# The low halves of attention's probabilities, taken for two quarters of a head in one operation

## The chip, the cores and the metric

The kernel runs on one core of one Trainium2 chip. The metric is the device time of one execution in microseconds (us), as the median of three runs.

## The reference, cut to what matters

A two-layer network of four sequences of 512 rows with 512 features each. Of its stages the change touches one, the cross attention of the second layer (16 heads of 32 features, 1024 keys, 4 sequences):

```
scores = einsum('bhsd,bhtd->bhst', Q, K) * scale
attn   = softmax(scores, axis=-1)
ctx    = einsum('bhst,bhtd->bhsd', attn, V)
```

All is float32 in the reference. Before this stage come the keys and values of the context, a first attention, a mixture of ternary experts and the queries; behind it come the output projection and a second mixture of experts.

## The kernel before, in words

The stages follow one another, each in a block of its own; a stage begins when every engine has left the one before. The change is in `attention_phase` (L1436 to L1800). It works through 4 sequences x 16 heads = 64 heads, each in 4 quarters, 256 steps in all. A head has 512 queries and 1024 keys.

**Two views of the scores.** For the maxima TensorE computes the scores with the queries on the partitions (`max_scores`, L1706, two matmuls of 512 columns for one quarter of the queries, into one of two places of `t_psM`), and VectorE takes their maximum (`maximum`, L1670, 128x1024). For the softmax it computes them again with the keys on the partitions (`scores`, L1725, one matmul for each of the quarter's two blocks of 128 keys, into two places of `t_psE`), now with the maxima as three more rows of the contraction. ScalarE takes the exponential of each block (L1632) into `t_e`, float32, a ring of 8 quarters.

**High and low halves.** `mix` (L1736) multiplies the probabilities with the values in bfloat16. The high half of a float32 number is read in place (`upper`, every second 16-bit word of `t_e`). The low half, the number less its high half, is computed by the function `halves` into `t_low`, with a subtraction of 128x1024 for one quarter. Quarters u = 0 and 2 are taken by GpSimd (L1591), u = 1 and 3 by VectorE (L1678). `mix` of a quarter has four matmuls: for each block one on the high and one on the low half.

**Order.** It is written by hand. In the step (h, u) TensorE issues `max_scores` for the quarter 28 steps on (EARLY), then for each of two blocks `scores` of the quarter 4 steps on (AHEAD) and `mix` of (h, u): 8 matmuls a step. VectorE issues in the step first `halves` of the quarter 3 steps on, if that is one of its own, and then the maximum of the quarter 28 steps on. GpSimd issues `halves` of the quarter 4 steps on, if that is one of its own. In the last 28 steps (7 heads) there are no more maxima to compute. `wait_free` (L1530) makes TensorE's `max_scores` wait until the maximum of the quarter that held its place of `t_psM` has been taken, which is the one two steps back.

**Groups.** Every 16 steps (4 heads) GpSimd splits the maxima of a group in three bfloat16 parts (`max_parts`, L1601, L1603, L1605, L1607, in the step h = 1, u = 1 of each four heads, behind that step's `halves`), and TensorE turns them (`max_transpose`, L1714, in the step h = 2, u = 1 of each four heads, ahead of that step's `max_scores`). The turned block takes a place of `t_psM` for itself, so that the `max_scores` behind it waits for the maximum of the step just before.

**Waits of `halves`.** GpSimd waits until VectorE has written its half that comes before in the order of quarters (`lo_dve`), and for the exponentials (`expd`). VectorE waits for the exponentials alone. `mix` of a quarter waits for its low half (`wait_lo`, L1482).

Of the kernel before, what the change touches and what calls it, by code (L numbers as in the profile page):

```python
# [6 lines left out]
BF16 = mybir.dt.bfloat16  # L7
ACT = mybir.ActivationFunctionType
ALU = mybir.AluOpType
# [1426 lines left out]
def attention_phase(nc, queries_dram, keys_dram, values_dram, mixed_dram, ident, qst, loaded, kst, vst, kv_loaded, ones_set):  # L1436
# [8 lines left out]
    TC = T // P  # L1445
    AHEAD, MAXAHEAD = 4, 7
    RING = 8
    LO_ON_POOL = (0, 2)
    NLD = 3
    mixed_v = mixed_dram.rearrange("b r (h d) s -> b h r d s", h=NH)  # L1450

    with ExitStack() as c:
        sb = lambda name, shape, dt: c.enter_context(nc.sbuf_tensor(name, shape, dt))
        sem = lambda name: c.enter_context(nc.semaphore(name))
        e32 = sb("t_e32", [P, RING, 2, S], F32)
        low = sb("t_low", [P, RING, 2, S], BF16)
# [13 lines left out]
        scored, expd = sem("t_scored"), sem("t_expd")  # L1470
        lo_dve, lo_pool = sem("t_lo_dve"), sem("t_lo_pool")
# [1 line left out]
        copied_out = sem("t_copied_out")  # L1473
        stored = [sem(f"t_stored{i}") for i in range(2)]

        def upto(quarters, head, u):

            return head * len(quarters) + sum(q <= u for q in quarters)

        LO_ON_DVE = tuple(u for u in range(4) if u not in LO_ON_POOL)  # L1480

        def wait_lo(eng, head, u):  # L1482
            pool = u in LO_ON_POOL
            eng.wait_ge(lo_pool if pool else lo_dve, upto(LO_ON_POOL if pool else LO_ON_DVE, head, u))

        def slot(h, u):

            return (h * 4 + u) % RING

        def upper(h, u):  # L1490

            return e32[:, slot(h, u), :, :].rearrange("p i s -> p (i s)").bitcast(BF16).rearrange(
                "p (i s w) -> p i s w", i=2, w=2)[:, :, :, 1]

        def ahead(b, h, u, n):

            h, u = h + (u + n) // 4, (u + n) % 4
            return b + h // NH, h % NH, u

        def steps(b):  # L1500
            return [(b, h, u) for h in range(NH) for u in range(4)]
# [7 lines left out]
        def within(b, h):  # L1509

            return not (isinstance(b, int) and b > LAST)

        def place_of_max(b, m):

            after = (m - LATE) // GROUP
            return m + (max(0, after) if isinstance(b, int) and b == 0 else after)
# [5 lines left out]
        def banks_of(place):  # L1522

            return psM[:, place % 2, :, :]
# [17 lines left out]
        def group_at(b, h, u, step):  # L1542

            if (4 * h + u) % GROUP == step:
                b2, h2, _ = ahead(b, h // G * G, 0, GROUP)
                if within(b2, h2):
                    return b2, h2 // G
            return None

        with nc.Block() as block:  # L1550
            @block.sync
            def _(sp):
                def load(b, g):
                    load_queries(sp, b, g, queries_dram, qst, loaded)
                    load_keys_values(sp, b, g, keys_dram, values_dram, kst, vst, kv_loaded)

                def put_max(b, g):

                    sp.wait_ge(n_copied, b * G + g + 1)
                    sp.dma_start(qst[KR:AR, g, :, :].rearrange("r h (u s) -> r (h u) s", u=4),  # L1560
                                 nrows[:, :]).then_inc(max_loaded[g], 16)

                def batch(b):
                    for h in range(NH):
                        if h % G == 1 and (due := group_at(b, h - 1, 0, 0)):
                            put_max(*due)
                        sp.wait_ge(copied_out, b * NH + h + 3)
                        sp.dma_start(mixed_v[bass.ds(b, 1), h].rearrange("o r d s -> (o r) d s"),
                                     ost[:, h % 2, :]).then_inc(stored[h % 2], 16)
                        if h % G == G - 1 and not (isinstance(b, int) and b == LAST):  # L1570
                            sp.wait_ge(mixed, (b * NH + h) * 4 + 4 + RING)
                            load(b + 1, h // G)

                for i in range(2):
                    sp.sem_inc(stored[i], 16)
                put_max(0, 0)
                for b in range(B):
                    batch(b)
                for i in range(2):
                    sp.wait_ge(stored[i], 16 * (B * NH // 2 + 1))  # L1580

            @block.gpsimd
            def _(pool):
                def halves(b, h, u):
                    head = b * NH + h
                    if u in LO_ON_POOL:
                        before = upto(LO_ON_DVE, head, u)
                        if not (isinstance(before, int) and before == 0):
                            pool.wait_ge(lo_dve, before)
                        pool.wait_ge(expd, head * 8 + 2 * u + 2)  # L1590
                        nc.gpsimd.tensor_tensor(low[:, slot(h, u), :, :], e32[:, slot(h, u), :, :], upper(h, u),  # L1591
                                                ALU.subtract).then_inc(lo_pool, 1)

                def max_parts(b, g):

                    k = b * G + g
                    pool.wait_ge(maxed, k * GROUP + GROUP)
                    if not (isinstance(b, int) and b == 0 and g == 0):
                        pool.wait_ge(n_xposed, k)
                    m, zeros = nmax[:, g % 2, :, :], nparts[:, 3, :, :]  # L1600
                    nc.gpsimd.tensor_tensor(nparts[:, 0, :, :], m, zeros, ALU.subtract).then_inc(n1_done, 1)  # L1601
                    pool.wait_ge(n1_done, k + 1)
                    nc.gpsimd.tensor_tensor(nrest[:, :, :], m, nparts[:, 0, :, :], ALU.subtract).then_inc(nrest_done, 1)  # L1603
                    pool.wait_ge(nrest_done, k + 1)
                    nc.gpsimd.tensor_tensor(nparts[:, 1, :, :], nrest[:, :, :], zeros, ALU.subtract).then_inc(n2_done, 1)  # L1605
                    pool.wait_ge(n2_done, k + 1)
                    nc.gpsimd.tensor_tensor(nparts[:, 2, :, :], nrest[:, :, :], nparts[:, 1, :, :],  # L1607
                                            ALU.subtract).then_inc(n3_done, 1)

                nc.gpsimd.memset(nparts[:, :, :, :], 0.0).then_inc(zeros_set, 1)  # L1610
                pool.wait_ge(zeros_set, 1)
                max_parts(0, 0)
                for n in range(AHEAD):
                    halves(*ahead(0, 0, 0, n))
                def batch(b):
                    for _, h, u in steps(b):
                        b2, h2, u2 = ahead(b, h, u, AHEAD)
                        if within(b2, h2):
                            halves(b2, h2, u2)
                        if due := group_at(b, h, u, SPLIT_AT):  # L1620
                            max_parts(*due)
                for b in range(B):
                    batch(b)
# [41 lines left out]
            @block.vector  # L1665
            def _(dve):
                def maximum(b, h, u):
                    m = 4 * h + u
                    dve.wait_ge(max_scored, b * 4 * NH + m + 1)
                    nc.vector.tensor_reduce(nmax[:, h // G % 2, h % G, u:u + 1],  # L1670
                                            banks_of(place_of_max(b, m)).rearrange("p a t -> p (a t)"),
                                            AX_X, ALU.max, negate=True).then_inc(maxed, 1)

                def halves(b, h, u):
                    head = b * NH + h
                    if u in LO_ON_DVE:
                        dve.wait_ge(expd, head * 8 + 2 * u + 2)
                        nc.vector.tensor_tensor(low[:, slot(h, u), :, :], e32[:, slot(h, u), :, :], upper(h, u),  # L1678
                                                ALU.subtract).then_inc(lo_dve, 1)

                for m in range(EARLY):
                    maximum(*ahead(0, 0, 0, m))
                    if m >= EARLY - AHEAD + 1:
                        halves(*ahead(0, 0, 0, m - EARLY + AHEAD - 1))
                def batch(b):
                    for _, h, u in steps(b):
                        b2, h2, u2 = ahead(b, h, u, AHEAD - 1)
                        if within(b2, h2):
                            halves(b2, h2, u2)
                        b2, h2, u2 = ahead(b, h, u, EARLY)  # L1690
                        if within(b2, h2):
                            maximum(b2, h2, u2)
                for b in range(B):
                    batch(b)
# [666 lines left out]
```

## Time and profile before

| | |
|---|---|
| median of 3 runs | 1772.18 us (1770.33 to 1776.66) |
| the profiled execution | 1772.23 us, its span 1770.4 us |
| PE busy | 1454.6 us (82%), 8465 matmuls |
| DVE busy | 1258.1 us (71%) |
| ACT busy | 970.7 us (55%) |
| POOL busy | 438.6 us (25%) |
| the attention stage | 778.5 to 1277.4 us |
| of it, steps with maxima at full rate | 830 to 1237 us |
| steps without maxima | 1237 to 1277.4 us |

PE is TensorE, DVE VectorE, ACT ScalarE, POOL GpSimd, SP the queue that issues DMAs. A row of the timeline gives the start of an instruction, its duration, engine, line of the code, operation, and what it writes and reads; in square brackets stands how long the engine was idle before it and who released it. "x2" merges two in a row. Matmuls overlap: one of 512 columns is recorded with 0.38 us, while the next starts 0.22 us behind it. Two VectorE operations in a row overlap in the record by some 0.08 us: a pair of maxima is recorded with 2.34 us, one alone with 1.21.

### The profile page before, as it was taken

The numbers are of one execution on the slowest core, as the hardware profiler recorded it, in microseconds if no ns is written. First come the engines' busy times: TensorE is split into PE (matmuls) and PEld (weight loads), VectorE is DVE, ScalarE is ACT, GpSimd is POOL, SyncE is SP. The second block draws the span as 40 slices with busy tenths as digits, with TensorE's granted clock in tenths as the row PEclk, the third lists the DMA queues.
The fourth block names the chain that finished last, engine by engine and source line by source line (L and its number), as shares of the span: only waits on it lengthen the run. The fifth ranks groups of instructions, "written<-read, shape, count | busy, mean of one in ns | idle before, by whom it ended". The sixth has DMA issues, their size and how long they took to land. (4 is left out here: it accounts for less than half of the span.)

```text
span 1770.4 us, 24758 instructions
## 1 busy us (share of the span) xinstructions
PE 1454.6 (82%) x8465; PEld 839.6 (47%) x8536; DVE 1258.1 (71%) x1520; ACT 970.7 (55%) x1440; POOL 438.6 (25%) x343
## 2 busy tenths in 40 slices
PE   4999988999551774878999999999826599999996
PEld 3554534555240333323555555555403366666663
DVE  4888856655582676859999999999448686655551
ACT  5878723344171555414777777767612376665551
POOL 0122210000313004304555555555752000000000
PEclk9999998999755996878999999999958699999998
DMA  6788650000083226420423233331177396666640
GB/s 220 244 276 290 204 205 1 0 0 0 1 354 111 72 90 186 111 79 11 97 74 95 76 92 79 90 81 28 36 213 226 115 327 219 219 220 219 220 142 28
DMA packets 145938, 236.92 MB, mean 134 GB/s; under 512 B 11320, under 2 KB 61496, under 8 KB 144704
## 3 DMA queue, kind: packets, MB, share of 16 engines
q1 hardware_dynamic: 140352, 210.65, 38.5%
q0 software_dynamic: 5504, 25.20, 3.9%
q8 instruction: 48, 0.79, 0.2%
q14 instruction: 34, 0.28, 0.1%
HBM read 169.74 MB, written 59.59 MB: 130 GB/s over the span
## 5 line engine op out<-in xcount | busy, mean ns | idle before, releaser
L1632 ACT ACTIVATE t_e<-t_psE 128x512 f32<-128x512 f32 x512 | 304.6, 597 | 133.6 <-PE t_psE L1725 124.9
L1670 DVE TENSOR_REDUCE t_nmax<-t_psM 128x1 f32<-128x1024 f32 x256 | 301.5, 1212 | 15.7 <-PE t_psM L1706 15.6
L1591 POOL TENSOR_TENSOR t_low<-t_e 128x1024 bf16<-128x1024 f32 x128 | 250.0, 1955 | 196.4 <-ACT t_e L1632 186.7
L1736 PE MATMUL t_psO<-t_e,vst 128*96 128x512 bf16 x512 | 200.6, 392 | 2.4 <-POOL t_low L1591 2.4
L1725 PE MATMUL t_psE<-qst,kst 99*128 99x512 bf16 x512 | 195.2, 382 | 0.1
L1736 PE MATMUL t_psO<-t_low,vst 128*96 128x512 bf16 x512 | 193.1, 377 | 0.0
L1678 DVE TENSOR_TENSOR t_low<-t_e 128x1024 bf16<-128x1024 f32 x128 | 177.9, 1390 | 18.3 <-ACT t_e L1632 17.8
L1706 PE MATMUL t_psM<-kst,qst 96*128 96x512 bf16 x512 | 164.0, 404 | 28.0 <-DVE t_nmax L1670 22.7
L2218 PE MATMUL e_psG<-xeT,e_w1p 128*128 (+1 forms) x1536 | 172.8, 276 | 9.4 <-DVE e_hT L2162 4.8
L2218 PEld LDWEIGHTS e_psG<-xeT,e_w1p 128*128 128x128 bf16 x1536 | 151.7, 99 | 30.9 <-issue 5.9
L2233 PE MATMUL e_psO<-e_w2p,e_hT 128*128 128x512 bf16 x752 | 164.9, 379 | 0.8
L2233 PEld LDWEIGHTS e_psO<-e_w2p,e_hT 128*128 128x128 bf16 x768 | 75.1, 98 | 88.9
L1736 PEld LDWEIGHTS t_psO<-t_e,vst 128*96 128x96 bf16 x512 | 84.1, 164 | 64.8 <-POOL t_low L1591 6.0
L1736 PEld LDWEIGHTS t_psO<-t_low,vst 128*96 128x96 bf16 x512 | 84.4, 165 | 27.4
L1706 PEld LDWEIGHTS t_psM<-kst,qst 96*128 96x128 bf16 x512 | 47.4, 99 | 94.0 <-DVE t_nmax L1670 47.2
L2114 ACT CAST e_w2p<-xres 128x2048 bf16<-128x2048 f32 x32 | 60.7, 1898 | 53.1 <-PE e_psO L2233 35.2
L642 PE MATMUL a_psR<-ctxN,a_pT 128*128 (+1 forms) x375 | 85.7, 384 | 4.3 <-DVE xres L555 3.9
L620 PE MATMUL a_psS<-ctxT,a_xT 128*128 (+1 forms) x375 | 87.8, 389 | 0.6 <-issue 0.2
L358 PE MATMUL c_psG<-ctxT,c_wT 128*128 128x512 bf16 x369 | 86.8, 383 | 1.0 <-issue 0.2
L115 POOL DMA_DIRECT2D ternary<-c_wout x48 | 41.7, 868 | 185.0 <-ACT c_wout L228 185.0
L2120 ACT ACTIVATE e_g<-e_psG,e_b1T 128x256 f32<-128x256 f32 x128 | 53.7, 470 | 59.5 <-PE e_psG L2218 40.7
L361 PE MATMUL c_psG<-c_wT,ctxT 128*128 128x512 bf16 x371 | 85.6, 379 | 0.7
(229 smaller groups left out, 2309.3 us busy)
## 6 DMA issues: line engine op xcount, KB each, us to landing
piece<-in_L_ffn_w SPq DMA_DIRECT2D x32, 1024.0 KB, 13.5
xres<-in_L_ffn_w SPq DMA_DIRECT2D x32, 1024.0 KB, 15.2
wT<-ternary POOLq DMA_DIRECT2D x8, 1536.0 KB, 21.4
kst<-keys SPq DMA_DIRECT2D x96, 128.0 KB, 4.2
mixed<-t_ost SPq DMA_DIRECT2D x64, 192.0 KB
c_rows<-in_ctx SPq DMA_DIRECT2D x8, 1024.0 KB, 10.3
xres<-in_L_ffn_wg SPq DMA_DIRECT2D x8, 1024.0 KB, 7.6
xres<-in_L_ffn_wu SPq DMA_DIRECT2D x8, 1024.0 KB, 7.1
```

Of the source, the lines that this page charges most:

```text
L358: last = nc.tensor.matmul(psG[:, k, :], wT[:, 0, a, k * P:(k + 1) * P], ctxT[:, b, q * 512:(q + 1) * 512], start=(i == 0), stop=(i == 11))
L620: last = nc.tensor.matmul(psS[:, par, h * 512:(h + 1) * 512], xT[:, par, ra * KC + k, :], ctxT[:, rb * KC + k, bass.ds(b * T + h * 512, 512)],
L642: last = nc.tensor.matmul(psR[:, :], pT[:, par, ra * TC + k, :], ctxN[:, bass.ds(b * TC + k, 1), rb, :].rearrange("p o d -> p (o d)"), sta ...
L1591: nc.gpsimd.tensor_tensor(low[:, slot(h, u), :, :], e32[:, slot(h, u), :, :], upper(h, u), ALU.subtract).then_inc(lo_pool, 1)
L1632: nc.scalar.activation(e32[:, slot(h, u), i, :], psE[:, i, :], ACT.Exp, scale=SC).then_inc(expd, 1)
L1670: nc.vector.tensor_reduce(nmax[:, h // G % 2, h % G, u:u + 1], banks_of(place_of_max(b, m)).rearrange("p a t -> p (a t)"), AX_X, ALU.max, ...
L1678: nc.vector.tensor_tensor(low[:, slot(h, u), :, :], e32[:, slot(h, u), :, :], upper(h, u), ALU.subtract).then_inc(lo_dve, 1)
L1706: last = nc.tensor.matmul(banks_of(place_of_max(b, m))[:, i, :], qst[0:KR, g, h % G, u * P:(u + 1) * P], kst[0:KR, g, h % G, i * 512:(i + ...
L1725: nc.tensor.matmul(psE[:, i, :], kst[:, g, h % G, k * P:(k + 1) * P], qst[:, g, h % G, :], start=True, stop=True).then_inc(scored, 1)
L1736: last = nc.tensor.matmul(psO[0:VW, h % 2, :], vst[:, g, 2 * u + i, :].rearrange("p (w h) -> p h w", h=G)[:, h % G, :], part[:, i, :], sta ...
L2218: last = nc.tensor.matmul(psG[:, g % 4, i, :], w1p[:, ra, k, f:f + P], xeT[:, rb * KC + k, ee, :].rearrange("p o s -> p (o s)"), start=(n ...
L2233: last = nc.tensor.matmul(psO[:, m, :], hT[:, ra, k, m * P:(m + 1) * P], w2p[:, rb, k, :], start=(k == 0 and i == 0), stop=(k == FC - 1 an ...
```

## The change

The subtraction takes two quarters at once. Those of u = 0 and 1 are computed by GpSimd in one operation of 128x2048, issued at the place of u = 1; those of u = 2 and 3 by VectorE in one, issued at the place of u = 3. The numbers computed are the same. `mix` of u = 0 and 1 waits for GpSimd's operation of the head, `mix` of u = 2 and 3 for VectorE's. GpSimd waits for VectorE's operation of the head before.

```diff
-    LO_ON_POOL = (0, 2)
...
-        def upto(quarters, head, u):
-
-            return head * len(quarters) + sum(q <= u for q in quarters)
-
-        LO_ON_DVE = tuple(u for u in range(4) if u not in LO_ON_POOL)
-
         def wait_lo(eng, head, u):
-            pool = u in LO_ON_POOL
-            eng.wait_ge(lo_pool if pool else lo_dve, upto(LO_ON_POOL if pool else LO_ON_DVE, head, u))
+            eng.wait_ge(lo_pool if u < 2 else lo_dve, head + 1)
...
+        def pair(h, u):
+
+            q = slice(slot(h, u), slot(h, u) + 2)
+            whole = e32[:, q, :, :].rearrange("p q i s -> p (q i s)")
+            return (low[:, q, :, :].rearrange("p q i s -> p (q i s)"), whole,
+                    whole.bitcast(BF16).rearrange("p (n w) -> p n w", w=2)[:, :, 1])
...
             def _(pool):
                 def halves(b, h, u):
                     head = b * NH + h
-                    if u in LO_ON_POOL:
-                        before = upto(LO_ON_DVE, head, u)
-                        if not (isinstance(before, int) and before == 0):
-                            pool.wait_ge(lo_dve, before)
-                        pool.wait_ge(expd, head * 8 + 2 * u + 2)
-                        nc.gpsimd.tensor_tensor(low[:, slot(h, u), :, :], e32[:, slot(h, u), :, :], upper(h, u),
-                                                ALU.subtract).then_inc(lo_pool, 1)
+                    if u == 1:
+                        if head >= 1:
+                            pool.wait_ge(lo_dve, head)
+                        pool.wait_ge(expd, head * 8 + 4)
+                        lows, whole, highs = pair(h, 0)
+                        nc.gpsimd.tensor_tensor(lows, whole, highs, ALU.subtract).then_inc(lo_pool, 1)
...
                 def halves(b, h, u):
                     head = b * NH + h
-                    if u in LO_ON_DVE:
-                        dve.wait_ge(expd, head * 8 + 2 * u + 2)
-                        nc.vector.tensor_tensor(low[:, slot(h, u), :, :], e32[:, slot(h, u), :, :], upper(h, u),
-                                                ALU.subtract).then_inc(lo_dve, 1)
+                    if u == 3:
+                        dve.wait_ge(expd, head * 8 + 8)
+                        lows, whole, highs = pair(h, 2)
+                        nc.vector.tensor_tensor(lows, whole, highs, ALU.subtract).then_inc(lo_dve, 1)
```

On VectorE, behind the 28 early maxima of the attention stage (t_nmax is the maximum, t_low the low halves). Before:

```order
L1678 TENSOR_TENSOR t_low<-t_e 128x1024
L1670 TENSOR_REDUCE t_nmax<-t_psM 128x1 x2
L1678 TENSOR_TENSOR t_low<-t_e 128x1024
L1670 TENSOR_REDUCE t_nmax<-t_psM 128x1 x2
L1678 TENSOR_TENSOR t_low<-t_e 128x1024
```

and of the changed kernel:

```order
L1668 TENSOR_REDUCE t_nmax<-t_psM 128x1 x28
L1677 TENSOR_TENSOR t_low<-t_e 128x2048
L1668 TENSOR_REDUCE t_nmax<-t_psM 128x1 x4
L1677 TENSOR_TENSOR t_low<-t_e 128x2048
L1668 TENSOR_REDUCE t_nmax<-t_psM 128x1 x4
```

Where an operation on one quarter stood ahead of every second maximum, an operation on two quarters now stands ahead of every fourth, that of the step u = 0.

On GpSimd, around one split of a group's maxima (t_nparts and t_nrest are its parts). Before:

```order
L1591 TENSOR_TENSOR t_low<-t_e 128x1024 x8
L1601 TENSOR_TENSOR t_nparts<-t_nmax,t_nparts 128x16
L1603 TENSOR_TENSOR t_nrest<-t_nmax,t_nparts 128x16
L1605 TENSOR_TENSOR t_nparts<-t_nrest,t_nparts 128x16
L1607 TENSOR_TENSOR t_nparts<-t_nrest,t_nparts 128x16
```

and of the changed kernel:

```order
L1590 TENSOR_TENSOR t_low<-t_e 128x2048 x4
L1599 TENSOR_TENSOR t_nparts<-t_nmax,t_nparts 128x16
L1601 TENSOR_TENSOR t_nrest<-t_nmax,t_nparts 128x16
L1603 TENSOR_TENSOR t_nparts<-t_nrest,t_nparts 128x16
L1605 TENSOR_TENSOR t_nparts<-t_nrest,t_nparts 128x16
```

The operation just ahead of the split is now the one on the quarters u = 0 and 1 of the head h = 2 of the four; before it was the one on its quarter u = 0 alone, and that on u = 2 stood behind the split.

## Rows read from the trace of the kernel before

**Rows 1.** Windows of the profile: the stretch with maxima, then the stretch without (times in us)
```profile
core 0: us, PE busy (x) PEld busy (x) DVE busy (x) ACT busy (x) POOL busy (x), PEclk, DMA share, GB/s
...
830.00:1237.00 407.00, 388.96 (x1769) 228.96 (x1768) 392.59 (x330) 289.14 (x507) 229.99 (x163) 1.00 0.32 78
1237.00:1277.40 40.40, 37.95 (x165) 22.69 (x164) 23.27 (x15) 32.16 (x58) 33.69 (x17) 1.00 0.13 34
```

**Rows 2.** Waits of PE within 830 to 1240 us: us in total, times, longest us
```profile
PE t_psM L1706 <- DVE t_nmax L1670: 18.0, 14, 1.3
```

**Rows 3.** Timeline, 900 to 912 us: two steps of an undisturbed head (start us, us, engine, line)
```profile
900.82 0.60 PE L1706 MATMUL t_psM<-kst,qst 96*128 96x512 bf16 x2
...
901.20 1.32 DVE L1678 TENSOR_TENSOR t_low<-t_e 128x1024 bf16<-128x1024 f32 x1
...
901.73 1.20 ACT L1632 ACTIVATE t_e<-t_psE 128x512 f32<-128x512 f32 x2 [0.56 <-PE t_psE L1725]
...
902.45 2.34 DVE L1670 TENSOR_REDUCE t_nmax<-t_psM 128x1 f32<-128x1024 f32 x2
902.58 0.60 PE L1706 MATMUL t_psM<-kst,qst 96*128 96x512 bf16 x2
...
903.07 1.89 POOL L1591 TENSOR_TENSOR t_low<-t_e 128x1024 bf16<-128x1024 f32 x1 [1.63 <-ACT t_e L1632]
903.23 0.39 PE L1736 MATMUL t_psO<-t_e,vst 128*96 128x512 bf16 x1
...
904.72 1.32 DVE L1678 TENSOR_TENSOR t_low<-t_e 128x1024 bf16<-128x1024 f32 x1
```

**Rows 4.** Timeline, 915 to 922 us: where a group of maxima is turned
```profile
915.28 1.32 DVE L1678 TENSOR_TENSOR t_low<-t_e 128x1024 bf16<-128x1024 f32 x1
...
915.49 1.20 POOL L1601 TENSOR_TENSOR t_nparts<-t_nmax,t_nparts 128x16 bf16<-128x16 f32 x1
...
917.35 0.21 POOL L1607 TENSOR_TENSOR t_nparts<-t_nrest,t_nparts 128x16 bf16<-128x16 f32 x1
917.52 1.89 POOL L1591 TENSOR_TENSOR t_low<-t_e 128x1024 bf16<-128x1024 f32 x1
...
918.42 0.60 PE L1706 MATMUL t_psM<-kst,qst 96*128 96x512 bf16 x2
...
918.80 1.69 DVE L1678 TENSOR_TENSOR t_low<-t_e 128x1024 bf16<-128x1024 f32 x1
...
920.18 0.22 PE L1714 MATMUL t_psM<-ident,t_nparts 128*128 128x128 bf16 x1
920.42 1.21 DVE L1670 TENSOR_REDUCE t_nmax<-t_psM 128x1 f32<-128x1024 f32 x1
...
921.69 0.61 PE L1706 MATMUL t_psM<-kst,qst 96*128 96x512 bf16 x2 [1.29 <-DVE t_nmax L1670]
```

**Rows 5.** Durations by line: ns min/median/max, first and last start us
```profile
L1678 DVE TENSOR_TENSOR t_low<-t_e x128: 1207/1323/2815, 813.4 to 1272.6; 128x1024 bf16<-128x1024 f32 x128
...
L1591 POOL TENSOR_TENSOR t_low<-t_e x128: 1887/1893/2918, 810.5 to 1272.9; 128x1024 bf16<-128x1024 f32 x128
...
L2154 DVE TENSOR_TENSOR e_w1p<-piece,e_w1p x32: 2284/2288/2294, 1410.7 to 1702.6; 128x2048 bf16<-128x2048 f32 x32
...
L1848 POOL TENSOR_TENSOR xres<-xres,o_bob x16: 1255/1256/3315, 1292.5 to 1315.4; 128x512 f32<-128x512 f32 x16
...
L1858 POOL TENSOR_TENSOR o_parts<-o_parts x2: 4808/4809/4810, 1333.7 to 1357.9; 128x2048 f32<-128x2048 f32 x2
```

**Rows 6.** Timeline, 1269 to 1274 us, in the stretch without maxima
```profile
1269.98 5.75 POOL L1591 TENSOR_TENSOR t_low<-t_e 128x1024 bf16<-128x1024 f32 x2 [1.16 <-DVE t_low L1678]
...
1272.95 0.47 PE L1736 MATMUL t_psO<-t_e,vst 128*96 128x512 bf16 x1 [0.60 <-POOL t_low L1591]
...
1273.26 0.38 PE L1736 MATMUL t_psO<-t_low,vst 128*96 128x512 bf16 x1
```

**Rows 7.** Windows of the profile, one stretch of the readout stage
```profile
605.00:615.00 10.00, 7.50 (x45) 3.83 (x44) 7.33 (x19) 6.17 (x12) 0.00 (x0) 1.00 0.24 79
```

## The prediction

> **What bounds the kernel now.** I read the profile from the coarse to the fine. The windows [rows 1] show that in the stretch with maxima (830 to 1237 us) TensorE is busy for 389.0 of 407 us and VectorE for 392.6, so either could set the pace, and that the granted clock is 1.00. The list of waits decides it: TensorE waits for VectorE's maxima 14 times, 18.0 us in all [rows 2], and 389.0 + 18.0 is the stretch. Between those waits it has no gap, so TensorE is the bound and VectorE is just fast enough. The waits come once in 16 steps, where a group is turned. In the last 28 steps (1237 to 1277.4 us) GpSimd is the busiest but for TensorE, 33.7 of 40.4 us [rows 1].
>
> The timeline of an undisturbed head gives the distances that I calculate with [rows 3]. A step begins with its first `max_scores` matmul and takes 902.58 - 900.82 = 1.76 us, 8 matmuls of 0.22. The step's first `mix` matmul comes 0.65 behind its begin (903.23). The exponentials made in a step (for the quarter 4 steps on) end at 901.73 + 1.20 = 902.93, 2.11 behind its begin. GpSimd takes them up at 903.07, or 2.25 behind the begin. VectorE takes up those of the next step at 904.72, 0.38 into the step that begins at 904.34. Its half and two maxima take 904.72 - 901.20 = 3.52 us, two of TensorE's steps.
>
> One more thing is in these rows: GpSimd's and VectorE's subtractions do not run at once. GpSimd's ends at 903.07 + 1.89 = 904.96, VectorE's has begun at 904.72 and takes 1.32 instead of the 1.21 that it takes at least [rows 3, 5]. At the turning an overlap of 0.61 (918.80 to 917.52 + 1.89 = 919.41) makes it 1.69, and GpSimd's first small split takes 1.20 us and ends at 916.69, just behind VectorE's half that ends at 916.60 [rows 4]. So whichever begins first holds the other nearly to its end. The Trainium skill ("GPSIMD Engine Reference", Key points) says that the two contend for SBUF interfaces where a VectorE instruction has two SBUF inputs; by that rule the trace agrees.
>
> **The prices.** On VectorE two halves of at least 1.21 become one of 128x2048. The same form stands in the last stage, f32 and bf16 in and bf16 out: 2.29 us [rows 5]. Two operations in a row overlap in the record by 0.08 (two maxima are 2.34, one 1.21), so the next begins 2.21 behind it: 0.05 less than two undisturbed halves (2 x 1.13), 0.29 less than the two as they run now (2 x 1.25, from 901.20 to 902.45). I take 2.21; its upper end is 2.27, twice the half. On GpSimd two of 1.89 become one, which no row shows. Twice the half is 3.79. The small splits of 16 elements take 0.21 [rows 4], which as a fixed part gives 0.21 + 2 x 1.68 = 3.57. A later stage has f32 additions of 512 elements at 1.26 and of 2048 at 4.81 [rows 5], 3.8 times as much: nearly all grows with the size. I take 3.70, with 3.57 and 3.79 as ends; the 4.81 is of all-f32 operands and is kept for a rival.
>
> **A plain head.** Count from the begin of step u = 0. Its VectorE operation used to be the half of u = 3 of the next head, and the maximum of the step began 1.25 later. Now the pair stands there. It can't begin earlier, since the exponentials of u = 3 are the last that it needs: it begins at 0.38, the maximum behind it at 0.38 + 2.21 = 2.59. TensorE goes on 1.27 behind the begin of the maximum that it waits for (920.42 to 921.69 [rows 4]), so at 3.86. The `max_scores` of step u = 2, which needs that place, is due at 2 x 1.76 = 3.52. Before, TensorE could have gone at 0.38 + 1.25 + 1.27 = 2.90, with 0.62 to spare. The 0.96 more gives a new wait of 0.34 us in every head. VectorE's work becomes less and its result later.
>
> GpSimd's pair needs the exponentials of u = 1. From the begin of the step that makes them it begins at 2.25 and ends at 5.95. Where TensorE waits for GpSimd it goes 0.05 behind its end (1269.98 + 2.92 = 1272.90, the longest of rows 5, to 1272.95), and its next matmul comes 0.31 behind instead of 0.22 [rows 6]: 0.14 in effect, so 6.09. The first `mix` that needs the pair is due three steps and 0.65 later, at 5.93. That lacks 0.16, but the wait of 0.34 for the maximum lies between the two and covers it. Before, the half of u = 0 had a step more and 1.81 us less to do.
>
> **At the turning** the `max_scores` of step u = 1 needs the maximum of step u = 0, and TensorE goes at 921.69 - 918.42 = 3.27 [rows 4]. With the pair it is 3.86. A second chain is as long: GpSimd's pair for that head begins at -(3 x 1.76 + 0.34) + 2.25 = -3.37 and ends at 0.33, and the split stands behind it instead of ahead. VectorE's pair begins at 0.38 and holds GpSimd until 2.67; before, the last split ended 0.96 behind VectorE's half (917.56 to 916.60), so it ends at 3.63. With 0.14 as above and 0.1 for the turning of 128 columns, TensorE goes at 3.87: 0.60 more than now. In that head no wait lies between the exponentials of u = 1 and `mix`, so the 0.16 is paid too. A group of four heads pays 0.60 + 0.16 + 3 x 0.34 = 1.8 us; 14 groups [rows 2] pay 25.
>
> **In the steps without maxima** a step is 6 matmuls, 1.33 us; the 7 heads take 40.4 us, 5.8 each [rows 1], since there too the two engines hold each other (GpSimd's longest is 2.92 against 1.89). With the pair: the second `scores` of a step begins at 0.66, its exponential ends some 0.48 + 0.60 later at 1.74, GpSimd at 1.88 + 3.70 = 5.58, TensorE goes at 5.72 and was due at 3 x 1.33 + 0.22 = 4.21. A head takes 5.32 + 1.51 = 6.8 us, 1.06 more; for the 6 heads whose exponentials fall here 6. TensorE would be busy for 78%. The readout stage holds the granted clock 1.00 at 75% busy [rows 7], so I add nothing for the clock.
>
> At the start the first pair must wait for two exponentials: about 1 us, once (an estimate: the exponentials of one more quarter, 1.20, of which some is covered). The 64 instructions fewer on each of two engines lie beside TensorE. No stage behind begins before attention ends, so the loss goes through whole. Sum: 25 + 6 + 1 + 0.3 for the 57th head = 32.5. Against the profiled execution's 1772.2 us, which is also the median shown, that is **1804.7 us**. With GpSimd at 3.57 a group pays 1.65 and the rest 6: 1801. With 3.79 and VectorE at 2.27 a plain head pays 0.40, a group 2.1, the rest 9: 1811.
>
> **Rivals.**
> - *Only the turnings and the end pay* (chance 0.13). The wait in the plain head rests on differences of a third of a microsecond. If they fall away, 14 x 0.76 + 7 remain: 1790 us. For it speaks that VectorE has slack in every head; against, that it can't begin before the exponentials, at which it already begins today.
> - *VectorE sets the pace and gets faster* (0.06). It is busy for 392.6 of 407 us. A head's two halves take 2.50, the pair 2.21: 57 x 0.29 = 16.5, and 14 times the 0.37 by which the half at the turning is stretched (1.69 against 1.32), 5: 1751 us. The point that decides is whether TensorE waits for maxima in plain heads; it never does now [rows 2], which speaks against. The Trainium skill ("VectorE: DVE Perf Modes", TRN2 errata) counts for this side: a large tile pays the fixed SBUF latency once, several small ones pay it each. By the rows it is 0.05 us a pair.
> - *GpSimd's pair is far slower* (0.05). At the 4.81 us of L1858 [rows 5] a head lacks 2.25 + 4.81 + 0.14 - 5.93 = 1.27 us, 57 x 1.27 = 72, the turnings 14 x 0.6 = 8, and the end 6 x 2.2 = 13: 1865 us. The low halves' own 1.89 for 1024 elements speaks against. The Trainium skill ("GPSIMD Engine Reference", Performance versus the Vector engine) measures 4.50 us for an f32 addition of 2048 elements; by it the result would be about 1848.
> - *All is hidden* (0.04): 1772 us.
>
> **How the numbers follow.** My forecast keeps 0.72. The range, 1786 to 1818, takes in its bounds and the first rival; above, 7 us are for the two engines holding each other by another 0.1 us in each head, which the ends of GpSimd's pair and the begin of VectorE's (within 0.1 of each other) leave possible. A measurement of this kernel tells about 0.3% (5 us) from no change: faster 0.06, within 0.04, slower 0.90.
>
> **What would show it.** In the changed profile TensorE should wait for t_nmax in every head with maxima, some 55 times, 0.3 us in plain heads and about 1.9 at turnings; VectorE's pair take 2.3 us and begin as the exponentials end; GpSimd's take 3.6 to 3.8; the last 28 steps take about 47 us with waits of 1.4 for t_low. I am wrong if plain heads stay at 7.04 us, if GpSimd's pair is above 4, or if the granted clock falls in this stage.

## The result, and the profile after

The changed kernel takes **1814.31 us** (median of 4 runs, 1812.01 to 1819.71), the kernel before beside it 1772.04 us: a ratio of 1.0239, 95% interval 1.0219 to 1.0260, or 42 us more. Forecast were 1804.7 us in a range of 1786 to 1818. The profiled execution took 1813.95 us, its span is 1812.1 us.

The costliest groups of the changed kernel that answer to the two subtractions and the maxima (line, engine, operation, what is written and read, count; then busy time, mean ns of one; then idle time before, and who ended it):

```profile
L1668 DVE TENSOR_REDUCE t_nmax<-t_psM 128x1 f32<-128x1024 f32 x256 | 303.8, 1219 | 49.3 <-PE t_psM L1704 49.2
L1590 POOL TENSOR_TENSOR t_low<-t_e 128x2048 bf16<-128x2048 f32 x64 | 230.4, 3600 | 239.5 <-ACT t_e L1630 239.5
...
L1677 DVE TENSOR_TENSOR t_low<-t_e 128x2048 bf16<-128x2048 f32 x64 | 151.9, 2374 | 41.7 <-ACT t_e L1630 41.7
```

GpSimd's pair takes 3.60 us, VectorE's 2.37 on average, and 2.29 where nothing holds it. VectorE's subtractions take 151.9 us in all, where 128 single ones at a mean of 1.39 us took 177.9. The waits of TensorE between 830 and 1270 us, to be held against the 14 waits of 18.0 us in [rows 2]:

```profile
PE t_psM L1712 <- POOL t_nparts L1605: 19.0, 13, 1.5
PE t_psM L1704 <- DVE t_nmax L1668: 11.5, 55, 0.5
```

The same matmul that waited 14 times now waits 55 times for a maximum, and at the turnings TensorE waits for the last split of the maxima (L1605) first. Two plain heads in the timeline of the changed kernel (start us, us, engine, line), which answer to [rows 3]:

```profile
904.79 0.38 PE L1734 MATMUL t_psO<-t_low,vst 128*96 128x512 bf16 x1
...
905.35 0.61 PE L1704 MATMUL t_psM<-kst,qst 96*128 96x512 bf16 x2 [0.17 <-DVE t_nmax L1668]
905.50 3.60 POOL L1590 TENSOR_TENSOR t_low<-t_e 128x2048 bf16<-128x2048 f32 x1 [3.50 <-ACT t_e L1630]
...
909.26 2.29 DVE L1677 TENSOR_TENSOR t_low<-t_e 128x2048 bf16<-128x2048 f32 x1 [0.29 <-ACT t_e L1630]
...
911.47 3.48 DVE L1668 TENSOR_REDUCE t_nmax<-t_psM 128x1 f32<-128x1024 f32 x3
...
912.18 0.38 PE L1734 MATMUL t_psO<-t_low,vst 128*96 128x512 bf16 x1
...
912.74 0.60 PE L1704 MATMUL t_psM<-kst,qst 96*128 96x512 bf16 x2 [0.19 <-DVE t_nmax L1668]
912.89 3.60 POOL L1590 TENSOR_TENSOR t_low<-t_e 128x2048 bf16<-128x2048 f32 x1 [3.79 <-ACT t_e L1630]
```

The last matmul of a step starts at 904.79 and the next `max_scores` at 905.35 instead of 0.22 behind it, which is 0.34 of loss (the profile counts 0.17 as idle, since it models the ends of matmuls). The same comes again 7.39 us later, at 912.74: a plain head takes 7.39 instead of 7.04 us. VectorE's pair begins at 909.26, 0.38 behind the begin of its step at 908.88 (905.35 + 2 x 1.76, to 0.01), lasts 2.29, the maximum follows 2.21 behind its begin (911.47), and TensorE goes 1.27 after that (912.74). Here is a turning, as in [rows 4]:

```profile
920.29 3.60 POOL L1590 TENSOR_TENSOR t_low<-t_e 128x2048 bf16<-128x2048 f32 x1 [3.80 <-ACT t_e L1630]
...
923.68 0.60 PE L1704 MATMUL t_psM<-kst,qst 96*128 96x512 bf16 x2
...
924.06 2.29 DVE L1677 TENSOR_TENSOR t_low<-t_e 128x2048 bf16<-128x2048 f32 x1 [0.29 <-ACT t_e L1630]
...
924.14 2.28 POOL L1601 TENSOR_TENSOR t_nrest<-t_nmax,t_nparts 128x16 f32<-128x16 f32 x1
...
926.27 1.22 DVE L1668 TENSOR_REDUCE t_nmax<-t_psM 128x1 f32<-128x1024 f32 x1
...
926.80 0.21 POOL L1605 TENSOR_TENSOR t_nparts<-t_nrest,t_nparts 128x16 bf16<-128x16 f32 x1
...
927.07 0.23 PE L1712 MATMUL t_psM<-ident,t_nparts 128*128 128x128 bf16 x1 [1.47 <-POOL t_nparts L1605]
...
927.54 0.61 PE L1704 MATMUL t_psM<-kst,qst 96*128 96x512 bf16 x2 [0.24 <-DVE t_nmax L1668]
```

The step u = 0 begins at 923.68. VectorE's pair begins at 924.06 and GpSimd's second small split, begun at 924.14, takes 2.28 us instead of 0.21 and ends as the pair has ended. The last split ends at 927.01, TensorE turns at 927.07 and goes on with `max_scores` at 927.54: 3.86 behind the step's begin, instead of 3.27.

In the last 28 steps TensorE waits five times for GpSimd's pair, and once, at the turning of the last group, for the split of its maxima (from 1270 us on):

```profile
PE t_psO L1734 <- POOL t_low L1590: 5.8, 5, 1.3
PE t_psM L1712 <- POOL t_nparts L1605: 1.8, 1, 1.8
```

In the kernel before this is the whole list from 1237 us on; the last turning makes TensorE wait for nothing there:

```profile
PE t_psO L1736 <- POOL t_low L1591: 2.4, 5, 0.8
```

Two of the waits for the pair in the changed kernel:

```profile
1290.53 0.38 PE L1723 MATMUL t_psE<-qst,kst 99*128 99x512 bf16 x1
...
1290.91 3.21 DVE L1677 TENSOR_TENSOR t_low<-t_e 128x2048 bf16<-128x2048 f32 x1 [3.07 <-ACT t_e L1630]
...
1292.03 0.47 PE L1734 MATMUL t_psO<-t_e,vst 128*96 128x512 bf16 x1 [1.11 <-POOL t_low L1590]
...
1295.04 3.60 POOL L1590 TENSOR_TENSOR t_low<-t_e 128x2048 bf16<-128x2048 f32 x1 [3.06 <-ACT t_e L1630]
...
1298.69 0.47 PE L1734 MATMUL t_psO<-t_e,vst 128*96 128x512 bf16 x1 [1.12 <-POOL t_low L1590]
```

A head takes 1298.69 - 1292.03 = 6.66 us there. VectorE's pair, begun at 1290.91 while GpSimd's still runs, takes 3.21. At the last turning the same happens, and the split is held in its turn:

```profile
1274.06 3.20 DVE L1677 TENSOR_TENSOR t_low<-t_e 128x2048 bf16<-128x2048 f32 x1 [3.14 <-ACT t_e L1630]
...
1275.07 2.27 POOL L1599 TENSOR_TENSOR t_nparts<-t_nmax,t_nparts 128x16 bf16<-128x16 f32 x1
...
1278.27 0.29 PE L1712 MATMUL t_psM<-ident,t_nparts 128*128 128x128 bf16 x1 [1.75 <-POOL t_nparts L1605]
```

The granted clock was forecast to stay at 1.00, and it did not. A piece of the timeline 2 us behind the turning at 958.5 us, and the granted clock (the third number from the end) in the window with it and in one behind it:

```profile
960.11 0.63 PE L1723 MATMUL t_psE<-qst,kst 99*128 99x512 bf16 x1
...
960.53 0.63 PE L1734 MATMUL t_psO<-t_e,vst 128*96 128x512 bf16 x1
...
960.96 0.63 PE L1734 MATMUL t_psO<-t_low,vst 128*96 128x512 bf16 x1
...
961.39 1.06 PE L1704 MATMUL t_psM<-kst,qst 96*128 96x512 bf16 x2
```

```profile
958.00:961.80 3.80, 3.09 (x10) 1.44 (x11) 2.11 (x2) 1.45 (x3) 0.61 (x3) 0.76 0.05 11
...
965.00:969.00 4.00, 4.00 (x20) 2.39 (x19) 3.71 (x3) 3.31 (x6) 0.12 (x1) 1.00 0.07 11
```

Here matmuls of 512 columns start 0.43 us apart instead of 0.22, and the granted clock is 0.76 on average over the first window, so TensorE went at its lower level (1.2 of 2.4 GHz) for a time. There are six such stretches of about 3 us between 830 and 1237 us, each behind a turning, and one of 5 us behind the turning of the last group (1278.27), 55 matmuls in all. There is none from 820 us to the end of the stage in the kernel before.

**Where the 42 us are**, by the first and last matmuls of the stage in the two profiles:

| | before | after | difference | forecast |
|---|---|---|---|---|
| first `max_scores` to first `mix` | 36.3 us | 37.1 us | +0.8 | +1 |
| first `mix` to last `max_scores` | 421.6 | 454.8 | +33.2 | +25.3 |
| last `max_scores` to last `mix` | 41.1 | 49.1 | +8.0 | +6.4 |
| the stage | 498.9 | 541.0 | +42.1 | +32.5 |

From turning to turning (16 steps) it is 29.68 us before. After, it is 31.40 us, and 33.0 in the groups with a stretch at the lower clock, so 1.7 for the waits and 1.6 more for the clock.

### The profile page after: what moved, and what is told of

Same layout as the page of the kernel before. It is cut to its first block and busy times, and to the rows that moved or that the text cites. A ratio compares the mean times of both kernels' runs of the same rounds, so it can differ in the third digit from the quotient of the medians.

```text
span 1812.1 us, 24566 instructions
## 1 busy us (share of the span) xinstructions
PE 1475.0 (81%) x8465; PEld 837.4 (46%) x8536; DVE 1246.7 (69%) x1456; ACT 972.6 (54%) x1440; POOL 436.1 (24%) x279
## 5 line engine op out<-in xcount | busy, mean ns | idle before, releaser
L1590 POOL TENSOR_TENSOR t_low<-t_e 128x2048 bf16<-128x2048 f32 x64 | 230.4, 3600 | 239.5 <-ACT t_e L1630 239.5
L1734 PE MATMUL t_psO<-t_e,vst 128*96 128x512 bf16 x512 | 205.1, 401 | 6.5 <-POOL t_low L1590 6.4
L1723 PE MATMUL t_psE<-qst,kst 99*128 99x512 bf16 x512 | 199.5, 391 | 0.1
L1734 PE MATMUL t_psO<-t_low,vst 128*96 128x512 bf16 x512 | 197.1, 385 | 0.0
L1677 DVE TENSOR_TENSOR t_low<-t_e 128x2048 bf16<-128x2048 f32 x64 | 151.9, 2374 | 41.7 <-ACT t_e L1630 41.7
```

Of the source, the lines that this page charges most:

```text
L1590: nc.gpsimd.tensor_tensor(lows, whole, highs, ALU.subtract).then_inc(lo_pool, 1)
L1677: nc.vector.tensor_tensor(lows, whole, highs, ALU.subtract).then_inc(lo_dve, 1)
L1723: nc.tensor.matmul(psE[:, i, :], kst[:, g, h % G, k * P:(k + 1) * P], qst[:, g, h % G, :], start=True, stop=True).then_inc(scored, 1)
L1734: last = nc.tensor.matmul(psO[0:VW, h % 2, :], vst[:, g, 2 * u + i, :].rearrange("p (w h) -> p h w", h=G)[:, h % G, :], part[:, i, :], sta ...
```

## The experiments

Each was timed beside the kernel before; the ratio is to it. The kernels take the low halves by a table for each head: engine, first quarter, number of quarters. What was changed in the table or in the order is shown. Their times as a whole carry some noise of the stages ahead: the attention stage's first matmul lies between 774 and 784 us in kernels that are the same up to there. So the stage's own length (first `max_scores` to last `mix` in the profile) is given too.

| kernel | median us | ratio, 95% interval | stage us | low clock matmuls |
|---|---|---|---|---|
| before | 1772 to 1774 | | 498.9 | 0 |
| changed | 1814.31 | 1.0239 (1.0219 to 1.0260) | 541.0 | 55 |
| GpSimd's pair only | 1861.41 | 1.0489 (1.0472 to 1.0507) | 589.4 | 99 |
| VectorE's pair only | 1811.47 | 1.0209 (1.0192 to 1.0226) | 537.0 | 50 |
| pairs, maximum first | 1763.45 | 0.9948 (0.9932 to 0.9965) | 490.5 | 0 |
| single quarters, maximum first | 1751.45 | 0.9875 (0.9859 to 0.9892) | 478.9 | 0 |
| pairs, singles in the last 7 heads | 1810.05 | 1.0204 (1.0172 to 1.0235) | 532.9 | 44 |
| VectorE's pair at turnings only | 1792.26 | 1.0107 (1.0078 to 1.0135) | 515.7 | 35 |
| VectorE's pair in plain heads only | 1791.62 | 1.0109 (1.0085 to 1.0132) | 517.5 | 0 |
| single quarters, maximum first, last 7 heads by VectorE | 1748.58 | 0.9871 (0.9844 to 0.9897) | 475.1 | 0 |

**1. GpSimd's pair only.**

```diff
-return [("pool", 0, 2), ("dve", 2, 2)]
+return [("pool", 0, 2), ("dve", 2, 1), ("dve", 3, 1)]
```

> GpSimd takes quarters 0 and 1 in one operation as in the changed kernel, VectorE quarters 2 and 3 one by one. Theory A (a late result in VectorE's order delays the maximum behind it, and the two engines hold each other): VectorE's half of u = 2 is due 5.66 us behind the begin of step u = 0, while GpSimd's pair runs from 4.01 to 7.61; it is held for about 1.9 us, the maximum behind it comes 1 us too late for TensorE, and a head takes 8 to 8.6 us: 1830 to 1860 us. Theory B (the loss comes from VectorE's long operation alone, GpSimd's pair lies beside other work): plain heads back at 7.04 us, 1772 to 1785 us.

Measured: 1861.41 us, the slowest of all. VectorE's half of u = 2 becomes due while GpSimd's pair runs (rows of this kernel's timeline):

```profile
904.71 3.60 POOL L1604 TENSOR_TENSOR t_low<-t_e 128x2048 bf16<-128x2048 f32 x1 [4.54 <-ACT t_e L1644]
...
906.86 2.53 DVE L1692 TENSOR_TENSOR t_low<-t_e 128x1024 bf16<-128x1024 f32 x1
...
909.32 1.21 DVE L1682 TENSOR_REDUCE t_nmax<-t_psM 128x1 f32<-128x1024 f32 x1
```

GpSimd's pair runs from 904.71 to 908.31; VectorE's half begins at 906.86 and takes 2.53 us instead of 1.21: held for 1.3 us, where 1.9 was expected. The maximum behind it starts at 909.32 only. TensorE's waits for maxima between 830 and 1325 us:

```profile
PE t_psM L1719 <- DVE t_nmax L1682: 58.5, 86, 2.0
PE t_psM L1727 <- DVE t_nmax L1682: 7.1, 14, 0.5
```

Theory A holds and B falls: GpSimd's pair is not beside other work. In the changed kernel it does little harm in plain heads, because VectorE's pair comes when GpSimd's has just ended (905.50 + 3.60 = 909.10, and 909.26, in the head shown above). A head takes about 8.7 us here, and 8.8 with its share of the lower clock, at which 99 matmuls went; 8 to 8.6 was expected, and the time lies just above the 1860 allowed.

**2. VectorE's pair only.**

```diff
-return [("pool", 0, 2), ("dve", 2, 2)]
+return [("pool", 0, 1), ("pool", 1, 1), ("dve", 2, 2)]
```

> VectorE takes quarters 2 and 3 in one operation as in the changed kernel, GpSimd quarters 0 and 1 one by one. Theory A: plain heads still wait 0.34 us for the maximum (7.39 us a head), the turning costs 0.6 more than before, the steps without maxima go back to about 5.7 us a head: 1795 us, and up to 1805 if the granted clock still falls behind turnings. Rival (GpSimd's pair makes the loss): 1772 us.

Measured: 1811.47 us, above the 1805 that I had allowed. From turning to turning it is 31.36 us, or 33.0 with a stretch at the lower clock, as in the changed kernel. So the 0.34 in plain heads and the turning's 0.6 come from VectorE's pair alone, and GpSimd's split, which here is done in time, is not needed for the loss at the turning. The waits of TensorE for maxima show it (830 to 1275 us):

```profile
PE t_psM L1719 <- DVE t_nmax L1682: 34.6, 56, 2.1
```

The excess over my 1795 is first in the clock: 50 matmuls at the lower level, 0.21 us each, are 10.7 us, which makes 1806. About half of the rest is at the turning of the last group, for which I had no term. VectorE's pair holds the split there, and TensorE waits 2.8 us for it, where the kernel before has no wait:

```profile
1282.09 2.90 DVE L1692 TENSOR_TENSOR t_low<-t_e 128x2048 bf16<-128x2048 f32 x1 [3.07 <-ACT t_e L1644]
...
1282.81 2.26 POOL L1613 TENSOR_TENSOR t_nparts<-t_nmax,t_nparts 128x16 bf16<-128x16 f32 x1
...
1286.01 0.23 PE L1727 MATMUL t_psM<-ident,t_nparts 128*128 128x128 bf16 x1 [2.80 <-POOL t_nparts L1619]
```

In the profile the stage is 38.1 us longer than before, and the median of the whole time 37.8, so nothing points to the stages ahead.

**3. and 4. The maximum first.** In VectorE's steps the two operations change places. Number 3 does it with the pairs, number 4 with single quarters as in the kernel before:

```diff
                     for _, h, u in steps(b):
-                        b2, h2, u2 = ahead(b, h, u, AHEAD - 1)
-                        if within(b2, h2):
-                            halves(b2, h2, u2)
                         b2, h2, u2 = ahead(b, h, u, EARLY)
                         if within(b2, h2):
                             maximum(b2, h2, u2)
+                        b2, h2, u2 = ahead(b, h, u, AHEAD - 1)
+                        if within(b2, h2):
+                            halves(b2, h2, u2)
```

> The changed kernel with VectorE's two operations of a step in the other order: the maximum first, then the low halves. Theory A (the loss is the place of the pair ahead of the maximum, not the pair): no wait for t_nmax in plain heads, and none at the turnings, where before had 14 x 1.29 = 18 us; left are GpSimd's late pair at the end (6 to 8 us) and 0.06 us a head: 1762 to 1768 us. Rival (the long operations themselves cost, by holding each other and the memory): 1795 us or more.

> The kernel before with VectorE's two operations of a step in the other order: the maximum first, then the low half. Theory A: the turning's wait of 1.29 us goes, 14 times: 1754 us. Rival (VectorE, 98% busy in this stretch, sets the pace): 1772 us, the waits moved to plain heads.

Measured: 1763.45 us with the pairs, 1751.45 with single quarters. Number 3 is as theory A said (1762 to 1768), number 4 is 2.5 us below its 1754, and both beat the kernel before: the intervals of both ratios lie below 1, though by less than 2%. The pair is as long as in the changed kernel, 2.29 and 3.60 us; only its place is another. The waits of TensorE in the stretch with maxima, in number 3 (830 to 1225 us) and in number 4 (830 to 1220 us), are the whole list:

```profile
PE t_psO L1749 <- POOL t_low L1604: 0.2, 1, 0.2
```

```profile
PE t_psM L1719 <- DVE t_nmax L1682: 0.4, 1, 0.4
```

From turning to turning it is 28.57 us with the pairs and 28.33 with single quarters, against 16 x 1.76 = 28.2 us of TensorE's own work. The 0.24 in four heads fit GpSimd's late pair, 0.06 a head, as worked out from 2.25 + 3.60 + 0.14 - 5.93. With this order the turning costs 0.1 us at most. VectorE was busy for 392.6 of 407 us in the kernel before, which is 96%, not the 98% of the expectation; in number 4 (830 to 1217 us) it is busy for 381.7 of 387 us, 99%, and TensorE for 386.7. So its busy time was no bound, only its order was.

**5. Single quarters at the end.**

```diff
-return [("pool", 0, 2), ("dve", 2, 2)]
+return [("pool", 0, 2), ("dve", 2, 2)] if head < 57 else [("pool", 0, 1), ("dve", 1, 1), ("pool", 2, 1), ("dve", 3, 1)]
```

> The changed kernel, but the last 7 heads (those without maxima beside them) take their low halves quarter by quarter as before. Theory: GpSimd's late pair costs about 1 us a head there, and the wait of 1.5 us in each head lets TensorE's clock fall once: 6 to 9 us less than the changed kernel, 1805 to 1808 us. Rival (the end is bound otherwise): 1814 us.

Measured: 1810.05 us, 4 less than the changed kernel where 6 to 9 were expected. The stage is 8.1 us shorter (532.9 to 541.0), the last `max_scores` to the last `mix` 40.5 instead of 49.1, and the low clock at the end is gone. The whole times alone don't show the gain: the intervals of the two ratios overlap (1.0172 to 1.0235, 1.0219 to 1.0260), so the rival's 1814 isn't excluded by them. The part at the end is shown by the profile. It holds both the waits for the pair and the wait at the last turning, which this version lacks too.

**6. and 7. VectorE's pair only at the turnings, and only elsewhere.**

```diff
+H = [("pool", 0, 1), ("dve", 1, 1), ("pool", 2, 1), ("dve", 3, 1)]
+D = [("pool", 0, 1), ("pool", 1, 1), ("dve", 2, 2)]
-return [("pool", 0, 2), ("dve", 2, 2)]
+return D if head % 4 == 2 else H
...
+return H if head % 4 == 2 else D
```

(The last line is number 7.)

> The kernel before, but in the head of each turning VectorE takes quarters 2 and 3 in one operation (GpSimd 0 and 1 one by one). Theory for the times: plain heads stay at 7.04 us, each turning waits 1.89 instead of 1.29 us: 14 x 0.6 = 8 us, 1781 us. For the clock: if the longer wait at the turning is what lets it fall, there are matmuls 0.43 us apart behind some turnings as in the changed kernel (50 of them, 11 us more: 1792 us); if it takes the waits of the plain heads too, there are none: 1781 us.

> The complement: VectorE takes quarters 2 and 3 in one operation in the three plain heads of each four, the head of the turning is as in the kernel before. Times: 43 x 0.34 = 15 us: 1788 us. For the clock: with the longest wait back at 1.29 us no matmuls 0.43 us apart, if the turning's wait decides; about 11 us more (1799 us) if the sum of the waits decides.

Measured: 1792.26 and 1791.62 us. The two have nearly the same sum of waits (26.6 and 28.3 us of TensorE for maxima) and differ in the longest. At the turnings only:

```profile
950.70 0.22 PE L1727 MATMUL t_psM<-ident,t_nparts 128*128 128x128 bf16 x1
...
951.53 1.22 DVE L1682 TENSOR_REDUCE t_nmax<-t_psM 128x1 f32<-128x1024 f32 x1
...
952.81 1.01 PE L1719 MATMUL t_psM<-kst,qst 96*128 96x512 bf16 x2 [1.89 <-DVE t_nmax L1682]
...
953.62 0.63 PE L1738 MATMUL t_psE<-qst,kst 99*128 99x512 bf16 x1
```

The wait is 1.89 us, and the matmuls behind it go 0.43 apart; this happened behind 4 of the 14 turnings with maxima and behind the last group's. From turning to turning it is 30.28 us, 0.60 more than before as expected, and 31.93 where the clock fell. The whole time met the expected 1792 partly by luck: 35 matmuls went at the lower clock, not 50, and the stretch behind the last `max_scores` is 1.6 us longer than before, which was not in the sum. In plain heads only:

```profile
922.89 0.22 PE L1727 MATMUL t_psM<-ident,t_nparts 128*128 128x128 bf16 x1
...
923.32 1.21 DVE L1682 TENSOR_REDUCE t_nmax<-t_psM 128x1 f32<-128x1024 f32 x1
...
924.59 0.60 PE L1719 MATMUL t_psM<-kst,qst 96*128 96x512 bf16 x2 [1.48 <-DVE t_nmax L1682]
```

The wait is 1.48 us (1.29 was expected; GpSimd's operation beside VectorE's half ends 0.2 later in the step), and from 820 us on no matmul of the stage goes at the lower clock. From turning to turning it is 30.94 us: 3 x 0.34 for the plain heads, and 0.2 for the turning. So with a wait of 1.9 us at the turnings the clock falls some of the times, and with many waits of 0.34 and one of 1.5 in each group it does not, at nearly the same sum. The total of number 7 is 4 us above my 1788, of which the 0.2 at each turning explains 3 and a wait of 0.8 at the last group's turning most of the rest.

**8. Single quarters, the maximum first, the last 7 heads by VectorE.** With number 4's order:

```diff
-return [("pool", 0, 1), ("dve", 1, 1), ("pool", 2, 1), ("dve", 3, 1)]
+return [("pool", 0, 1), ("dve", 1, 1), ("pool", 2, 1), ("dve", 3, 1)] if head < 57 else [("dve", u, 1) for u in range(4)]
```

> The kernel before with the maximum ahead of the low half in VectorE's order, and the low halves of the last 7 heads all by VectorE, quarter by quarter. VectorE's four halves take 4.5 us a head, less than TensorE's 5.3, and nothing holds it there: up to 3 us less than with the maximum first alone, 1748 to 1751 us. Rival (ScalarE's exponentials bound the end): no difference.

Measured: 1748.58 us. The last `max_scores` to the last `mix` is 37.0 instead of 40.8 us in number 4, which is 28 steps at TensorE's own 1.33. As a whole it can't be told apart from number 4 with certainty (ratios 0.9871 and 0.9875); in the profile the stage is 3.8 us shorter. It is the fastest version, 1.3% below the kernel before.

## Why the prediction was right, and by how much it was short

- **The plain heads: right.** 0.34 us a head was forecast from 0.38 + 2.21 + 1.27 - 3.52, and the profile after has each of these terms to 0.01. Number 2 shows that VectorE's pair alone makes it, number 3 that the length costs this only in the place ahead of the maximum.
- **The turnings: right in size, by another term.** 0.60 more was forecast and is there (30.28 to 29.68 in number 6, and 3.86 to 3.27 in the timeline). I held GpSimd's split to be as late as the maximum; in the profile after the maximum is the later by some 0.3 us (926.27 + 1.27 against the turning at 927.07), and number 2, without the late split, has the same 0.6. In what I added for GpSimd's pair I took 3.70; it is 3.60, near the lower end of 3.57. So the 0.16 there is 0.06, and a group costs 1.7 instead of 1.8. The printed terms of the sum (25, 6, 1 and 0.3) add up to 32.3; unrounded (14 x 1.78, 6 x 1.06) they give 32.6.
- **The steps without maxima: right for a head, the sum partly by luck.** 6.66 us a head against 6.8, by the same 0.1 of GpSimd's pair. The 8.0 us of the table hold 2.7 of the lower clock (13 matmuls), so the waits are 5.3, forecast 6.4. They are not all of the forecast kind: the waits for the pair grew from 2.4 to 5.8 us, or 3.4, and 1.8 are the wait for the split at the last turning, for which the prediction has no term. It stands in place of one head's wait for the pair. Number 3 has it too (1.8), so it comes from the pairs and not from the order; the kernel before has no wait there, and number 5, with single quarters at the end, one of 0.2 us.
- **The clock: wrong.** The step that failed is "The readout stage holds the granted clock 1.00 at 75% busy [rows 7], so I add nothing for the clock". I looked at the share of busy time in 10 us, and only for the last steps. The busy share did not decide it: between 830 and 1237 us TensorE is busy for 379 of 407 us, 93%, and the clock fell behind 6 of 14 turnings there and once at the end. What had changed is the loss at the turning, from 1.29 to about 1.9 us (1.47 idle ahead of the turning, 0.24 behind it, and the turning between), and numbers 6 and 7 show that this one matters and the plain heads' waits don't. 55 matmuls at 0.43 instead of 0.22 us are 11.8 us. With them my 32.5 becomes 44, and without the 2 to 3 us that I had too much it is the measured 42. A fall of the granted clock was among the signs by which the prediction called itself wrong. The waits alone come to 30 us, or 1802, close to the forecast; that 1814 still lies in the range is luck, since the room above was kept for the two engines holding each other.
- **The rivals.** "Only the turnings and the end pay" fell: 55 waits for maxima. "All is hidden" fell with the time. "VectorE sets the pace and gets faster" fell by number 4, which runs at TensorE's pace with all of VectorE's old work. "GpSimd's pair is far slower" fell: 3.60 us. The Trainium skill's figure of 4.50 us for an f32 addition of this size ("GPSIMD Engine Reference", Performance versus the Vector engine) is of other operands; here one input and the output are bfloat16, and the trace decides.
- **A wrong word.** The prediction calls VectorE's operation of step u = 0 the half of u = 3 "of the next head". It is that of the same head, three steps on. The distances are unaffected, since they were read in the timeline.

VectorE's work did become less, by 26 us in its subtractions (mostly because GpSimd seldom holds it now), and that was worth nothing, since VectorE's work did not bind.

## What to carry to other kernels

An engine that is 96% busy need not be the bound; look at what the waiting engine waits for, and at what stands ahead of that operation in the producer's order. A longer operation delays everything behind it on its engine by the length that it has more, so put the result that another engine will need first ahead of it: changing the order of two operations gave 20 us in the stage here, where merging operations lost 42. And count a new wait not only by its own length: behind waits of 1.9 us the matmuls lost a further 1.6 us, in some four of ten cases. Look last at what else a longer operation holds: here a split of 16 elements, at the one turning that has no maxima beside it.

## What the runs showed of the hardware

- **Two-input operations on GpSimd and VectorE, read from SBUF, exclude each other almost fully.** VectorE's half beside GpSimd's pair took 2.53 instead of 1.21 us (number 1), its pair 3.21 instead of 2.29, and GpSimd's split of 16 elements 2.28 instead of 0.21. The Trainium skill ("SBUF — State Buffer", Terms) describes the shared port pair as an exclusive lock held for the full instruction; the traces agree to within 0.15 us, by which the one held ends earlier than if it had begun behind the other. Maxima read from PSUM were never held (1.20 to 1.23 us throughout).
- **TensorE's clock fell behind single long waits.** Where a turning lost 1.9 us the granted clock went to 0.50 (1.2 of 2.4 GHz) for some 3 us in 6, 6, 6 and 4 of 14 cases (the changed kernel, numbers 2, 5 and 6), with TensorE at over 90% busy; where it lost 1.29 or 1.48 us (the kernel before, number 7) in none of 14 each. In number 1, with waits of 0.5 and 2.0 us around each turning, it was 11 of 14. At the last turning a wait of 1.75 us had such a fall in the changed kernel and none in number 3. Why it takes some turnings and not others stays open, and also whether what counts is the one wait or all idle time close around it; no run separates these.
- **GpSimd's subtraction grows with the size.** 1.89 us for 1024 elements and 3.60 for 2048, so 1.67 ns an element and a fixed part of 0.2.
